# Successive tiles of h at a pitch of 2064 bytes in place of 2048, in a graph layer with a full adjacency matrix on one TensorE

## The reference

```python
h = jnp.maximum(_layernorm(x, axis=-1), 0.0)      # x: 4096 x 256, float32
agg = jnp.matmul(adj, h)                          # adj: 4096 x 4096, float32, mostly zeros
out = jnp.matmul(agg, W.T) + b                    # W: 256 x 256
return x + jax.nn.relu(out)
```

## Time and profile before

| | |
|---|---|
| time, median of 2 runs | 384.27 us (384.17 to 384.37) |
| the profiled execution's own time | 383.73 us |
| its span, first to last instruction | 381.9 us |
| TensorE matmul busy | 376.7 us, 99% of the span |
| TensorE granted clock over the span | 1.00 |
| weight loads busy, beside the matmuls | 308.1 us |
| VectorE, ScalarE, GpSimd busy | 218.1, 170.3, 63.6 us |
| matmuls of add_up (L370) | 1536, busy 255.0 + 137.9 us |
| moved by DMA | 80.25 MB |

### The profile page before, as it was taken

The page is one execution under the profiler, slowest core; times in us unless marked ns, Lnnn a source line. Parts: engine busy times, 40 slices in busy tenths (PEclk is TensorE's granted clock), DMA queues, the critical chain, the costliest instruction groups (busy, mean ns, idle before and its releaser), DMA issues.

```text
span 381.9 us, 4421 instructions
## 1 busy us (share of the span) xinstructions
PE 376.7 (99%) x1649; PEld 308.1 (81%) x1649; DVE 218.1 (57%) x292; ACT 170.3 (45%) x196; POOL 63.6 (17%) x79
## 2 busy tenths in 40 slices
PE   8999999999999999999999999999999999999996
PEld 4788888888888888888888888888888888888885
DVE  4999999995744444444564444444465444444424
ACT  4565556564544343333543333334364334343414
POOL 2787777770010000000001000000000100000000
PEclk9999999999999999999999999999999999999999
DMA  7987787768649565656565856565656675656203
GB/s 239 356 279 264 266 264 257 211 212 322 195 148 349 194 193 193 194 193 203 181 197 189 311 185 197 187 202 185 200 186 206 234 255 187 205 182 205 68 2 110
DMA packets 22774, 80.25 MB, mean 210 GB/s; under 512 B 2464, under 2 KB 2976, under 8 KB 22752
## 3 DMA queue, kind: packets, MB, share of 16 engines
q1 hardware_dynamic: 20736, 72.36, 57.5%
q0 software_dynamic: 2016, 7.60, 5.5%
HBM read 75.76 MB, written 4.19 MB: 209 GB/s over the span
## 4 chain that ended last, share of the span: by engine, by line
PE 96%; DMA 2%; DVE 1%; SPq 1%; ACT 0%; issue 0%
PE bank L370 90%; PE bank L416 6%; DMA x_sb<-x_dram 2%; DVE adj_lo L215 0%; SPq L148 0%; SPq L145 0%; ACT out_sb L346 0%; DVE stats L231 0%; SPq L155 0%; DVE out_sb L284 0%; DVE centred L242 0%; DVE mean_var L236 0%
## 5 line engine op out<-in xcount | busy, mean ns | idle before, releaser
L370 PE MATMUL bank<-adj_hi,h_sb 128*128 128x512 f32 x1024 | 255.0, 390 | 0.0
L215 DVE TENSOR_TENSOR adj_lo<-adj_in,adj_hi 128x1024 fp32r<-128x1024 f32 x127 | 155.4, 1224 | 138.7 <-ACT adj_hi L306 138.7
L370 PEld LDWEIGHTS bank<-adj_hi,h_sb 128*128 128x128 f32 x1024 | 192.2, 188 | 41.0 <-ACT h_sb L317 1.1
L306 ACT ACTIVATE adj_hi<-adj_in 128x1024 fp32r<-128x1024 f32 x127 | 134.5, 1059 | 159.9 <-PE bank L370 157.9
L370 PE MATMUL bank<-adj_lo,h_sb 128*128 128x512 f32 x512 | 137.9, 390 | 0.5 <-DVE adj_lo L215 0.5
L370 PEld LDWEIGHTS bank<-adj_lo,h_sb 128*128 128x128 f32 x512 | 95.9, 188 | 21.3 <-DVE adj_lo L215 1.0
L195 POOL TENSOR_TENSOR rstd<-var_eps,minus_half 128x1 f32<-128x1 f32 x32 | 50.0, 1564 | 2.5
L207 POOL DMA_DIRECT2D out_t_dram<-out_sb x3 | 2.2, 723 | 209.8 <-DVE out_sb L284 209.8
L317 ACT ACTIVATE h_sb<-centred,rstd 128x256 fp32r<-128x256 f32 x32 | 16.3, 508 | 26.7 <-POOL rstd L195 26.6
L231 DVE BATCH_NORM_STATS2 stats<-x_sb 128x6 f32<-128x256 f32 x32 | 13.5, 421 | 4.0 <-DMA x_sb<-x_dram 4.0
L284 DVE TENSOR_TENSOR out_sb<-out_sb,xt_sb 128x512 f32<-128x512 f32 (+1 forms) x17 | 11.1, 659 | 7.6 <-ACT out_sb L346 7.6
(11 more groups left out here) (20 smaller groups left out, 29.0 us busy)
## 6 DMA issues: line engine op xcount, KB each, us to landing
adj_in<-adj_t_dram SPq DMA_DIRECT2D x127, 512.0 KB, 3.7
xt_sb<-x_t_dram POOLq DMA_DIRECT2D x4, 1024.0 KB, 7.3
x_sb<-x_dram SPq DMA_DIRECT2D x7, 512.0 KB, 6.4
out_t_dram<-out_sb POOLq DMA_DIRECT2D x3, 1024.0 KB, 5.0
out_t_dram<-out_sb SPq DMA_DIRECT2D x3, 256.0 KB, 2.0
adj_in<-adj_t_dram SPq DMA_DIRECT2D x2, 256.0 KB, 4.1
x_sb<-x_dram SPq DMA_DIRECT2D x2, 128.0 KB, 3.0
x_sb<-x_dram SPq DMA_DIRECT2D x1, 256.0 KB, 5.8
```

Source lines behind the costliest of these rows:

```text
L215: nc.vector.tensor_tensor(adj_lo[:, k, :], adj_in[:, k, :], adj_hi[:, k, :].bitcast(fp32), ALU.subtract).then_inc(s_lo, 1)
L306: nc.scalar.activation(adj_hi[:, k, :], adj_in[:, k, :], ACT.Copy).then_inc(s_hi, 1)
L370: last = nc.tensor.matmul(bank(g, kb, c)[:], h_sb[:, t, hp, kb * P:(kb + 1) * P], adj_parts[ap][:, n % U, chunk(c)], start=(t == 0 and (hp ...
```

## The change

The tile axis of h_sb gets four more elements (16 bytes) a tile, and the code reaches both parts of h through a helper that cuts them out of the longer row. Tile t of h then stands at offset 16t to the moving operands, modulo 512: the 32 tiles take each multiple of 16 from 0 to 496 once. h_sb grows by 32 x 16 = 512 bytes, so adj_in, adj_hi, adj_lo, agg_hi and agg_lo move up by exactly 512 bytes and keep their place modulo 512. The offset of w stays at 224.

```diff
+    STEP = 4
+
...
-        h_sb = sb("h_sb", [P, TILES, 2, D], fp32r)
+        h_sb = sb("h_sb", [P, TILES, 2 * D + STEP], fp32r)
...
+        def h_part(t, hp):
+            return h_sb[:, t, hp * D:(hp + 1) * D]
+
...
-                nc.vector.scalar_tensor_tensor(out=h_sb[:, t, 1, :], in0=centred[:, k, :],
+                nc.vector.scalar_tensor_tensor(out=h_part(t, 1), in0=centred[:, k, :],
                                                scalar=rstd[:, k:k + 1],
-                                               in1=h_sb[:, t, 0, :].bitcast(fp32),
+                                               in1=h_part(t, 0).bitcast(fp32),
                                                op0=ALU.mult, op1=ALU.subtract).then_inc(s_hlo, 1)
...
-                nc.scalar.activation(h_sb[:, t, 0, :], centred[:, k, :], ACT.Copy,
+                nc.scalar.activation(h_part(t, 0), centred[:, k, :], ACT.Copy,
                                      scale=rstd[:, k:k + 1]).then_inc(s_hhi, 1)
...
-                        last = nc.tensor.matmul(bank(g, kb, c)[:], h_sb[:, t, hp, kb * P:(kb + 1) * P],
+                        last = nc.tensor.matmul(bank(g, kb, c)[:], h_part(t, hp)[:, kb * P:(kb + 1) * P],
                                                 adj_parts[ap][:, n % U, chunk(c)],
```

## The result

The changed kernel takes 391.42 us (median of 2 runs, 391.36 to 391.48) against 384.27: 1.019 times as long, 95% interval 1.018 to 1.021. That is clear of noise; whether it is more than 2% can't be told. The prediction was 394. The profiled execution took 391.48 us with a span of 389.7.

The account below looks back on a forecast made before the run. TensorE bounds the kernel: number of matmuls times distance between starts. 1488 shifted matmuls at 6.67 ns more add 9.9 us to 384.27, giving 394.2, stated as 394 us; other parts were priced at nothing; range 376 to 402.

Parts of the forecast that it names:

- The mechanism: In add_up, the weight block's offset from the moving operand sets matmul distance: 226.7 ns at 0, 233.3 at 224.
- the list of signs: Profile after: tile 0 at 226.7 ns, tile 14 and product at 233.3, h durations unchanged, 89.5 us per 384 distances.
- The case of no effect: Rival: something other than offset makes w's 233; add_up stays at 226.7 ns, time at 384.3 us; chance 0.18.
- the likeliest case: All 31 shifted add_up tiles take the product's distance: 9.9 us more, 394 us, own range 390 to 399; chance 0.42.
- the graded case: Rival: add_up's excess grows with distance from offset 0, reaching 6.67 ns at 224; 5.9 us, 390.1 us; chance 0.16.
- the half-width row: Half-width matmuls at offset 224 stand 118.2 ns apart for 106.7 ns of columns, an excess of 11.5 ns.
- the bound of 398.7: Upper bound for shifted add_up tiles: half-width excess doubled to 23 ns, distance 236.4, 14.4 us more, 398.7 us.
- the faster case: Rival: most shifted add_up tiles lose a collision at offset 0 and save 9.8 us, 374.5 us; chance 0.16.
- the early stretch of rows 9 and 10: First tiles at offset 0 run at 232.5 ns after waits, so 226.7 wants offset and timing to fit; weaker evidence.

Follow-up runs that it names:

- all_at_224: Kernel before with 288 unused bytes between h_sb and adj_in, so every weight block of h stands at offset 224: 393.78 us, ratio 1.026.
- w_at_0: Kernel before with 224 unused bytes ahead of centred, so w comes to offset 0 from agg and h stays at 0: 383.40 us, ratio 0.998.
- all_at_16: Kernel before with the whole of h 16 bytes in, pitch 2048, every tile at offset 16: ratio 1.006 (1.002 to 1.009).

## Why the prediction was right, and where it wasn't

**What is shown.** The mechanism is the one forecast: 233.3 ns in all_at_224 by moving the adjacency alone, 226.7 in w_at_0 for the product with w left in place and agg moved, while add_up, moved as a whole, kept its pace. The two readings that carried the forecast, the product's distance and the 397 ns of the matmul beside which w is loaded, were read rightly; so was the claim that transfers and the other engines have no part. Tile 0 stayed at 226.7 inside its group, tile 14 followed the product at 2.80 us for twelve, the product stayed at 233.3, the writers of h at 505 and 478 ns, each as the list of signs said. The case of no effect is out, and the Trainium skill's "TensorE: Matmul & The Clock Gate", section "Step-by-step: what each phase is for", doesn't fit here where it says that a weight load takes no read bandwidth from the running matmul: with fp32r 6.7 ns a matmul hang on where the block stands that is loaded beside it. With bfloat16 the run agrees, since no offset showed.

**The term that was mis-sized.** 1488 matmuls at 6.67 ns made 9.9 us; measured are 7.4 us in add_up, 5.0 ns a shifted matmul. Of 31 shifted tiles five are cheap (1, 16 and 17 throughout, 15 and 31 after about four dear distances at their start) and four cost about half (11, 12, 27, 28). The rest lie around the product's distance, 2.78 to 2.81 us for twelve distances (231.7 to 234.2 ns each). Taking one sample for 31 was right in kind and a third too high; with a circle of 256 bytes in mind, tile 16 would have been counted among the cheap ones. Nothing in the trace of before could show that circle. I had allowed that some tiles keep 226.7, which is where the likeliest case's own lower end of 390 came from. The time alone would not have borne the forecast out: 391.42 is nearer to the graded case's 390.1 than to 394, and it lies below the 392.0 from which the prediction counted a result as slower. It is the rows of single tiles that decide between the cases.

**Where the reasoning was wrong though the number held.** Two slips in counting change nothing: the 14.28 us near the end hold 63 distances and not 64, and 14.28 / 63 is the 226.7 that the prediction states; and the 9504 bytes between w_hi and h_sb hold seven small tensors and not six. Three steps were wrong in substance. First, the half-width row. I read its 11.5 ns as an offset cost on half the columns, took an upper bound of 236.4 from it, and concluded that 226.7 might hold a part that a better offset removes. At offset 0 those matmuls stand 119.1 apart, no better than at 224. They say nothing about the full width, and neither the bound of 398.7 nor this support for the faster case had a ground. Second, the faster case itself: at none of the 32 offsets, nor at the finer ones, did four distances in a row go below 226.7 each by more than the rounding of the start times (0.90 us for four was the least). No offset tried took anything off the 13.3 ns. The figure of the Trainium skill's same page, section "Back-to-back issue gap" (columns and 2.5 ns, 215.8), is what the bfloat16 run measured; for fp32r no run here came near it. Third, the graded case: the cost doesn't grow with the distance from 0. It is full at 32 bytes and falls again at 176.

**The phase.** I took the early stretch of rows 9 and 10 as a sign that 226.7 needs the right timing as well, and called it weak. It was the better clue: the runs with waits, with alternating tiles and at offset 16 all show a stream with two states. At offset 0 it finds the cheap one back in four to seven distances, at 16 it may stay out for a whole group, and with a dear tile between every two cheap ones it is back only for the last part of each cheap tile.

**What stays open.** What it is that collides, and why the circle is 256 bytes. The runs show it with the 4-byte type and 512 columns, not with bfloat16, and not at 256 columns for offsets 0 and 224; they don't show the parts inside. What shorter loads do was seen only in streams of two lengths. Why one offset can hold either pace, and what sets it off in some runs and not in others, isn't shown. Why tiles 11, 12, 27 and 28 are cheaper isn't explained.

## What to carry to other kernels

Where TensorE is the bound, read the distance from start to start and compare stretches of the same shape: two values for one shape are a question worth a trace, and placement in a partition is one possible answer. In fp32r streams of this shape keep weight blocks and moving operands at the same place modulo 256 bytes, exactly the same and not merely near it (at 16 bytes the time came out 0 to 5 us longer from run to run), and place small tensors so that they don't shift one against the other; in bfloat16 it didn't matter. Judge such a stream in steady state and over several runs, since a wait ahead of it may decide its pace.

## What the hardware showed that I had not expected

- The same offset gives two paces: 233.3 ns through group 0 and 226.7 for the following 384 matmuls (all_at_16), and three levels of time between runs of one kernel, 384.1, 386.8 and 389.1 us.
- The cost repeats every 256 bytes: 1.000 (0.999 to 1.001) with every second tile at 256.
- Making a third of the weight loads smaller made the stream slower: 229.4 ns with those at 64 columns, 226.7 with all at 128.
- fp32r costs 13.3 ns a matmul above its columns at best, bfloat16 2.5.
